# A Mamba-style block and a 16-expert layer on one core: two blocks in front of the first keys, weighted queries one turn later, gathers with a lead of five

## The reference

```python
xn = _layernorm(x, axis=-1)
x = x + attn(xn, ...) + ffn(xn, ...)

# attn: a state-space block, 4 heads, chunks along the sequence
K = _rope(Bn[:, :, None, :] + B_bias, theta); Q = _rope(Cn[:, :, None, :] + C_bias, theta)
S1 = einsum(Qc, Kc) * g1c * decay; S2 = einsum(Qc, Kpc) * g2c * decay
y_intra = S1 @ xc + S2 @ xpc                      # inside a chunk
y_inter = einsum(Qc, exp(ell), Hprevs)            # from the carried state
y = (y_intra + y_inter + D * x) * silu(z); return y @ W_out

# ffn: 16 experts, the two best of each token, SwiGLU, layer norm per expert
h = jax.nn.silu(xf @ W1[ei]) * (xf @ W3[ei]); y = h @ W2[ei]
y = (y - mu) * rsqrt(var + EPS) * gamma[ei] + beta[ei]
out = out + combine[:, ei:ei + 1] * y
```

## Time and profile before

| | us |
|---|---|
| median of 3 runs | 275.35 |
| lowest and highest | 275.08 and 276.93 |
| the profiled execution, whole | 277.72 |
| its span, first to last instruction | 276.0 |

### The profile page before, as it was taken

How to read it: one execution, slowest core, us unless ns; L and a number is a source line. 1 busy time by engine, 2 the same in 40 slices (tenths; PEclk the granted TensorE clock), 3 DMA queues, 4 the chain that set the end, 5 groups by cost and what they waited for, 6 DMA issues and landing times.

```text
span 276.0 us, 7214 instructions
## 1 busy us (share of the span) xinstructions
PE 245.0 (89%) x2091; PEld 216.0 (78%) x2094; DVE 222.7 (81%) x596; ACT 146.2 (53%) x492; POOL 205.7 (75%) x279
## 2 busy tenths in 40 slices
PE   2999997499999999999999999999999999998500
PEld 0857964498998898899989979997998899887300
DVE  4768998967979989896989879699889787976446
ACT  1765989546464463737354654636362746452033
POOL 8658997846898979788897978898688786656300
PEclk9999999779999999999999999999999999999855
DMA  6630836976869979878898988788889688870195
GB/s 160 208 114 8 269 119 197 290 200 171 239 224 236 297 219 299 285 226 237 242 285 238 288 255 241 252 239 257 276 238 300 198 269 243 250 200 21 33 296 145
DMA packets 68278, 60.48 MB, mean 219 GB/s; under 512 B 6544, under 2 KB 52240, under 8 KB 68240
## 3 DMA queue, kind: packets, MB, share of 16 engines
q1 hardware_dynamic: 65680, 54.78, 67.1%
q0 software_dynamic: 2560, 5.25, 6.5%
HBM read 55.22 MB, written 4.78 MB: 217 GB/s over the span
## 4 chain that ended last, share of the span: by engine, by line
PE 74%; DMA 6%; ACT 6%; POOL 6%; issue 3%; DVE 2%; SPq 1%; ACTq 0%; POOLq 0%; DVEq 0%
PE bank L897 19%; PE bank L942 10%; PE bank L892 5%; PE bank L838 5%; PE bank L830 4%; ACT decay L1063 3%; PE bank L865 3%; PE bank L813 3%; DMA decay<-l_dram 3%; PE bank L715 3%; PE bank L783 2%; PE bank L820 2%; PE bank L856 2%; PE bank L788 2%; PE bank L938 2%
## 5 line engine op out<-in xcount | busy, mean ns | idle before, releaser
L897 PE MATMUL bank<-blkT,w_up 128*128 128x128 f32 x512 | 65.2, 281 | 1.0 <-ACT blkT L1113 0.8
L897 PEld LDWEIGHTS bank<-blkT,w_up 128*128 128x128 f32 x512 | 61.8, 197 | 2.0 <-issue 0.7
L654 POOL DMA_INDIRECT res_dram<-xrow,sidx x40 | 42.1, 1052 | 20.5 <-DVE xrow L1451 14.0
L597 POOL DMA_INDIRECT blk<-xn_dram,gidx x40 | 42.6, 1066 | 9.3 <-issue 7.0
L942 PE MATMUL bank<-w,xrow 128*128 128x128 f32 x256 | 34.7, 278 | 1.2 <-DVE xrow L1438 1.2
L942 PEld LDWEIGHTS bank<-w,xrow 128*128 128x128 f32 x256 | 31.1, 192 | 2.5 <-issue 2.5
L1119 ACT ACTIVATE xrow<-bank 128x512 f32<-128x512 f32 x40 | 24.4, 609 | 16.3 <-PE bank L897 6.7
L1423 DVE TENSOR_TENSOR xrow<-xrow,bank 128x512 f32<-128x512 f32 x40 | 27.2, 680 | 5.5 <-issue 4.4
L1349 DVE SCALAR_TENSOR_TENSOR kq<-sd,rms,bias_kq 128x512 f32<-128x512 f32 x32 | 22.7, 751 | 6.3 <-issue 5.2
L1113 ACT ACTIVATE blkT<-bank 128x128 f32<-128x128 f32 x40 | 11.5, 287 | 27.9 <-PE bank L883 22.5
L647 POOL TENSOR_TENSOR rstd<-mv,mhalf 128x1 f32<-128x1 f32 x40 | 24.5, 613 | 0.7 <-DVE mv L1435 0.5
(11 more groups left out here) (244 smaller groups left out, 613.5 us busy)
## 6 DMA issues: line engine op xcount, KB each, us to landing
w_up<-in_L_ffn_W_dram SPq DMA_DIRECT2D x96, 256.0 KB
w<-in_L_ffn_W_dram SPq DMA_DIRECT2D x48, 256.0 KB
e_row<-e_dram SPq DMA_DIRECT2D x12, 256.0 KB
decay<-l_dram SPq DMA_DIRECT2D x4, 512.0 KB, 5.7
gam<-in_L_ffn_gamma_dram SPq DMA_DIRECT2D x32, 64.0 KB
shift_y<-in_L_ffn_beta_dram SPq DMA_DIRECT2D x32, 64.0 KB
acc<-in_L_attn_u_dram SPq DMA_DIRECT2D x4, 256.0 KB, 3.7
xn_dram<-xrow SPq DMA_DIRECT2D x4, 256.0 KB, 5.0
```

What stands on the lines that cost most here:

```text
L597: g.indirect_dma_start(out=blk[:, b % SLOTS, :], out_offset=None, in_=xn_dram, in_offset=bass.IndirectOffsetOnAxis(ap=gidx[:, entry(b):ent ...
L654: g.indirect_dma_start(out=res_dram, in_=res[:, b % HALF, :], in_offset=None, out_offset=bass.IndirectOffsetOnAxis(ap=sidx[:, entry(b):ent ...
L897: last = m(bank[out][:, c * P:(c + 1) * P], w_up[:, u % SETS, n, c * P:(c + 1) * P], blkT[:, b % 2, :], start=True, stop=True)
```

## The change

1. **Experts of the blocks.** `pick_experts` leaves DVE. ACT compares with two sign functions that also sum along the row, POOL combines the sums in four small instructions, PE transposes the result after the fourth of its eight decay sums, and DVE copies it to `blk_e` inside `one_hots(0)`.
2. **POOL before the turns.** 8 products of 256 columns take the place of 16 of 128. The first `square_own` moves behind four gathers. `gather(0)` stands in front of the eighth `cut_rows`.
3. **Turn 0.** PE executes two matmuls whose result nobody reads (`WARM_BLOCKS`), then transposes and multiplies blocks 0 and 1 and does `down(0)`, and only then transposes the first keys and queries; `turn_kq` is split into `turn_k` and `turn_q`. DVE scales the first mean squares in front of the row numbers, makes three of the four theta parts in a row, and writes `product(0)` in front of `rotate(0)`. ACT squares tile 0 after two instead of four of its late decay tiles, copies block 0 before it loads the table for silu and sine, and weights the values after block 2.
4. **Every later turn on POOL.** `weigh_q(t - 1)` stands in turn t, behind `rms_pow(t)` and `finish`; where it does, the gather goes behind `rot_sine`. Gathers run with `LEAD = 5`. Turn 1 and part of turn 2 have an order of their own. SP loads the decay row of tile t - 1 in turn t.
5. Keys and queries are weighted in the other half of the scratch tile `sd`.

```diff
+    LEAD = 5
+    WARM_BLOCKS = 2
-    CUT = (0, 1, 3, 2)
+    CUT = (0, 1, 2, 3)
-        bn_kq = sd[:, 0:2, :]
+        bn_kq = sd[:, 2:4, :]
...
@@ sync @@
             for t in range(NT):
+                if t > 3 and takes(t - 1):
+                    load_row(t - 1)
                 for b in blocks_of(t):
-                    if t > 2 and takes(t) and b == blocks_of(t)[0]:
-                        load_row(t)
                     for u in sets(b):
                         load(u)
+            load_row(NT - 1)
@@ gpsimd @@
+            pool.wait_ge(counted, 1)
+            g.tensor_scalar(behind[0:NU], full_n[0:NU], NE - 0.5, -2.0 * NE, ALU.is_gt, ALU.mult)
+            link(g.tensor_tensor(full_n[0:NU], full_n[0:NU], mix_n[0:NU], ALU.add))
+            link(g.tensor_tensor(full_n[0:NU], full_n[0:NU], behind[0:NU], ALU.add))
+            g.tensor_scalar(full_n[0:NU], full_n[0:NU], 2.0 * NE, 2.0 * (NE - 1), ALU.add, ALU.min)\
+                .then_inc(expert_ready, 1)
-            for t in range(NT):
+            for t in range(0, NT, 2):
...
-            square_own(0)
-            for t in range(SUMMED, NT):
+            for t in range(SUMMED, NT - 1):
                 cut_rows(t)
             pool.wait_ge(xn_out, 16 * NBATCH)
             pool.wait_ge(gidx_ready, 1)
+            gather(0)
+            cut_rows(NT - 1)
...
             def iteration(t, first, second, blocks):
                 b0, b1, b2 = blocks
-                if first and t > 0:
+                if t < 2:
+                    (begin, second_tile)[t]()
+                    return
+                if first:
                     rms_pow(t)
                 if b0 is not None:
                     finish(b0 - 2)
-                    gather(b0 + SLOTS)
-                if first and t > 0:
+                if takes(t - 1):
+                    weigh_q(t - 1)
+                elif b0 is not None:
+                    gather(b0 + LEAD)
+                if first:
                     rot_sine(t)
...
                 if b0 is not None:
+                    if takes(t - 1):
+                        gather(b0 + LEAD)
                     store(b0 - 2)
...
-                if first:
-                    weigh_q(t)
@@ tensor @@
+            def begin():
+                pe.wait_ge(sidx_ready, 1)
+                for _ in range(WARM_BLOCKS):
+                    m(bank[6][:, :], ident[:, :], xnT[:, 0:512], start=True, stop=True)
+                turn_block(0)
+                pe.wait_ge(theta_ready, 2)
+                rise(0)
+                turn_block(1)
+                rise(1)
+                turn_block(2)
+                down(0)
+                turn_block(3)
+                turn_k(0)
+                state_product(0)
+                turn_q(0)
@@ scalar @@
+            act.wait_ge(ends_ready, 1)
+            a(cmp_f[0:NU], ends[0:NU], ACT.Sign, scale=-1.0, bias=at_full[0:NU, 0:1], accum_out=full_n[0:NU, 0:1])
+            a(cmp_m[0:NU], ends_l[0:NU], ACT.Sign, scale=-1.0, bias=from_mix[0:NU, 0:1], accum_out=mix_n[0:NU, 0:1])\
+                .then_inc(counted, 1)
...
+            def begin():
+                absolutes(0)
+                out_block(0)
+                nc.scalar.preload_act_table_set("silu_and_others")
+                act.wait_ge(rest_in, 16 * RESTS)
+                sines(0)
+                silu(0)
+                out_block(1)
+                silu(1)
+                out_block(2)
+                weigh(0)
+                move_x(0)
+                gates(0)
+                out_kq(0)
@@ vector @@
             one_hots(0)
-            pick_experts()
             one_hots(1)
+            mean_square(0)
...
+            def begin():
+                cut_turns(0)
+                cut_turns(1)
+                cut_turns(2)
+                dve.wait_ge(rest_in, 16 * RESTS)
+                dve.wait_ge(theta_psum, 1)
+                weigh_bc(0)
+                norm_kq(0)
+                cut_turns(3)
+                rot_cosine(0)
+                product(0)
+                rotate(0)
+                product(1)
+                norm_y(0)
+                diagonal(0)
+                diagonal(1)
```

More of the change, by code:

```diff
@@ L960, in iteration @@
                     down(b0 - 1)
-                if first and not begins:
+                if first:
                     project_bc(t)
@@ L964, in iteration @@
                     project_out(t - 2)
[L965 removed]
+                if b0 is not None:
                     rise(b0)
```

199 lines of the change are left out of this document (98 added, 101 removed).

## The result

The changed kernel takes **280.23 us** (median of 4 runs, 280.06 to 281.98). The kernel before, run beside it, takes 276.14 us (4 runs, 275.08 to 277.88). The ratio is 1.015, with a 95% interval of 1.009 to 1.021: slower by 4.1 us, and the interval leaves open whether the loss reaches 2%. I had forecast 272.1 with a range up to 276.5, so the prediction was wrong in its direction.

What follows compares the result with a forecast made beforehand. It took PE as the limit in the turns (not alone), not at the start, and a POOL and DVE chain at the end. Start -3.4, turns +0.5, end -0.3 gave -3.2: 275.35 to 272.1 us; range 268.8 to 276.5.

Steps and rivals of the forecast that it cites:

- Start, -3.4 us: Up to turn 1's mixed `rise`: earlier gather and full clock bring it at 59.6 to 59.7 instead of 63.13; bounds -2.0, -4.5.
- The hold of the second key instruction: DVE's keys in turns with `qs`: POOL's `qs` gets in between the two key instructions; the second ends 1.1 us late.
- Turns, +0.5 us: All later turns: moving `weigh_q` costs 0.5 us in sum, bounds -1.8 (no hold) and +8.
- Turns 2, 6, 10, 14, "+0.4 each": These turns: nothing gained in front, `product` 1.1 us later at 82.2 against 81.8 wanted; +1.6 us for four.
- Turns 4, 8, 12, "-0.35 each": These turns: `mean_square` 0.86 us early, `qs` hold 1.1 us late; PE pays 0.25, is spared 0.59; -1.0 us together.
- Odd turns, "0": Turns 3, 7, 11, 15: a third block, `product` ended 0.9 us before it was wanted, so no cost.
- The rival "slower": Turns: `qs` holds up both key instructions, keys 1.7 us late, PE pays 8.2 us; 279.9 us, chance 0.10.
- No hold: Turns: `qs` does not hold the key instructions, so the turns gain 1.8 us; 269.8 us, chance 0.18.
- The start gains little: Start: late row numbers, landing slow as before, low clock for `rise(0)`; gain only 1.5 us; 274.0 us, chance 0.22.
- End, -0.3 us: From block 38 on: `weigh_q(15)` behind the power hides only the step through DVE; bounds 0 and -1.0.
- The calibration: Whole kernel: profiled execution to median; the median lies 2.4 us below the profiled one, and this difference was applied.

Runs made afterwards that it cites:

- undo_move: Changed kernel with POOL's query weighting back at the end of its own tile's turn and the gather before the sine products; new start and lead of five kept: 273.86 us.
- lead_six: Changed kernel with the query weighting done by DVE instead of POOL, and a gather lead of six in place of five: 270.89 us.
- gather_first: Changed kernel with the turn's first gather placed on POOL ahead of the query weighting instead of behind the sine products: 293.83 us.
- pool_product: Changed kernel with DVE weighting the queries and an idle POOL product of two constant SBUF tiles where the weighting stood: 281.97 us.
- pool_iota: Changed kernel with DVE weighting the queries and an idle POOL iota, which reads nothing, where the weighting stood: 270.57 us.
- only_move: Kernel before with only the query weighting moved into the next turn, before the sine products; old start and lead of six kept: 282.75 us.
- no_warm: Changed kernel with DVE weighting the queries, without the two throw-away PE products ahead of the first block: 269.69 us.

## Why the prediction was wrong

**Start, -3.4 us: right in sum, in part by luck.** It gave 3.38 us to the mark of turn 1. Within it the gather came at 45.18, not 44.4, the late end of my bounds. The second table was complete at 42.59, 1.5 us earlier than before and not 2.8, since DVE came to the last write of the first table 1.2 us later (34.90 against 33.66). `mean_square(0)`, which I had suspected, did no harm, because the row numbers had to wait for PE's product of the tables, until 43.22:

```profile
42.52 0.59 DVE L1371 TENSOR_SCALAR ms<-ms 128x2 f32<-128x2 f32 x1
42.65 0.57 PE L817 MATMUL bank<-blk,rot 128*128 128x40 f16 x16 [0.84 <-DVE rot L1382]
```

From gather to first transposition it took 4.0 us, as forecast. The second `rise` then ended at 56.04, 0.6 us later than I had it, and what follows up to the mixed `rise` took 3.8 us instead of my 4.2; the two misses cancel in most part. The clock stayed up, and the wait for `product(0)` was there. In `undo_move` the start gave 4.3 us, in the other kernels with it between 3.4 and 4.6, and only 1.8 in the profiled execution of `lead_six`.

**The hold of the second key instruction: right in size, on a wrong ground.** I took it 1.1 us late with 1.8 us for the instruction. Measured: 1.02 us, and 1.76 us for the second key instruction of turn 3. But I had derived it from taking turns, one instruction each, and `gather_first` shows that this isn't so: the hold stayed short only since POOL had to stop behind `qs`.

**Turns, +0.5 us: the step that failed**, at +7.33 us. Three terms of it were mis-sized.

- *Turns 2, 6, 10, 14, "+0.4 each".* Measured +0.28, +0.97, +0.97, +0.75. I compared the late `product` with the moment at which PE wants it, and that part was right: the `rise` grew by 0.35 us. But I stopped there. The remaining 0.5 to 0.6 us arise at `state_product`, since the whole rest of DVE's turn is late. DVE has little slack in these turns, and a wait of 1 us in it is not absorbed by one instruction's slack.
- *Turns 4, 8, 12, "-0.35 each".* Measured +1.28 and +1.08 in turns 4 and 8 (turn 12 +0.74). The 0.86 us that `mean_square` was to gain were not gained, because POOL was in a store in front of the power; POOL's own list was the later of the two. And there the first key instruction was held, 1.46 us for the pair.
- *Odd turns, "0".* Measured +0.32 in turn 7, and +1.45 in turn 3, where the new order puts one more store in turn 2, so that the power for a block comes late (DVE waits 1.52 us for it), `mean_square` and the keys behind it too, and the second half of the `rise` waits 0.95 us. I had named the slack of 0.9 us at `product`, not the power in front of it.

**The rival "slower"** gave 279.9 us, close to the result, and I gave it 0.10. Its list of what PE pays was nearer than mine, and the closeness of the sum is in part luck. Its mechanism (both key instructions held, 1.7 us late everywhere) holds in part for turns 4, 8 and 12 alone. The line in it that outweighs the rest, "from 0.34 us per turn on", was the warning: I had written that less than half a microsecond per turn decides, and still gave it a tenth.

**No hold** is wrong: `pool_product` against `pool_iota` shows the hold with nothing else changed. **The start gains little** is wrong too.

**End, -0.3 us:** +0.25 by the cut, 0.0 at the last store. The hold met `shift_block` in place of the wait for the power. It is the same error: a POOL product that is moved meets the next DVE instruction with two SBUF inputs.

**The calibration** (profiled execution against median) added little: span +4.2, medians +4.1.

**What stays open:** why the first key instruction is held in turns 4, 8 and 12 and the second in the others. The starts are alike: keys 0.81 to 0.83 us behind the power, `qs` 0.38 to 0.41 us behind the keys. What differs is DVE's idle time ahead of it, 0.95 to 0.97 against 0.37 to 0.42 us. `only_move` shows the same split. In `pool_product` the idle time in turns 4, 8 and 12 is 0.38 us, and there the second key instruction is held (2.43 us for the pair), so it isn't the kind of turn. No run changes the idle time alone.

## What to carry to other kernels

Before moving a POOL instruction that reads SBUF, list what DVE does in that stretch. The first DVE instruction there with two SBUF inputs can be held until POOL's unbroken row ends; those that read PSUM were not held in these runs. A DVE instruction with one SBUF input isn't safe by that alone: `mean_square` was held for up to 1.4 us (`undo_move`, turn 3). Where two engines are both nearly full, price a delay by the turn and not by the next consumer: here PE paid nearly the whole hold in turn 6 and a third of it in turn 7. And if POOL's product takes 1.3 us and DVE's 0.7, as here, DVE may be the cheaper place even when it is the busier engine.

## What the runs showed of the hardware

- A DVE instruction that the profile shows as started was kept out by POOL instructions whose recorded start is later (76.29 against 76.63), and through three of them in a row: 3.13 us for an instruction of 0.35. The same shows in the old kernel, where a rotation took 2.19 us until the second of two sine products was done. By recorded starts it isn't always the first one that wins, and the two sides don't take turns. The Trainium skill (the page and section named above) says that issue order decides who blocks; by the starts in the profile this isn't so here, and no run shows the order of issue itself.
- POOL is slowed too. Its product takes 1.48 us in turns where the first key instruction gets in, and 1.25 to 1.27 where it doesn't.
- Behind a pause of 1.44 us of PE the granted clock fell to 0.50 (`no_warm`). Behind one of 1.33 us it stayed at 1.00 in the changed kernel and fell to 0.50 in `lead_six`, with the same instructions ahead of it. One profile doesn't tell which of the two levels the next execution gets.
